# Edge stage: how gathers are released, in what size the one-hot rows are made, and which engine does the small chain steps

## Chip, core, metric

One Trainium2 chip, one of its cores. The metric is device time in microseconds (us) of one execution of the program, the median of three: 3991.97 us (3991.55 to 4013.34). Five engines run their own instruction streams and meet at semaphores: TensorE (PE), VectorE (DVE), ScalarE (ACT), GpSimd (POOL), and SyncE (SP), which here only issues DMAs.

## What is computed

A graph layer over 6250 nodes and 206,250 edges sorted by destination, then attention over all nodes (mix) and eight small expert networks. The change touches only the edge part:

```python
h = (x @ W.T).reshape(n, H, D)                       # 8 heads of 32
alpha = einsum('ehd,hd->eh', h[src], a_src) + einsum('ehd,hd->eh', h[dst], a_dst)
enc = relu(edge_attr @ edge_W.T + edge_b).reshape(-1, H, D)
alpha = alpha + sum(enc * h[dst], axis=-1)
alpha = where(alpha >= 0, alpha, 0.2 * alpha)
amax = segment_max(alpha, dst, num_segments=n)
ex = exp(alpha - amax[dst])
denom = segment_sum(ex, dst, num_segments=n)
out = segment_sum(h[src] * (ex / maximum(denom[dst], 1e-10))[..., None], dst, num_segments=n)
```

## The kernel before

Stages run one after the other: start (node rows, index lists), key/value and mix (both also gather some source rows ahead of time into `scratch_pre_rows`), edges, combine, experts. The edge stage is `stage_edges`. Edges come in groups of 256 (`GE`); a **turn** takes two groups that fall into one block of 64 destination nodes each, 512 edges; there are 452 turns (`D`), and 8 of them (`KW`) make a **window**, for which the maxima of the scores are chained from turn to turn and rescaled. k is a turn's place in its window, 0 to 7.

What a turn d does, and where:

- SP loads the destination rows of its two groups (`table`, ring of `RL` = 3 turns, so turn d's load waits until `spread_out(d - 3)` is done), for every second turn a pair of edge features and of destination numbers repeated on all partitions (`feat`, `relb`: `load_pair(g)` for turns 2g and 2g+1, ring of 2 pairs), and for each window six transfers (`load_window`) and two small ones (`load_turns`). For 124 of the 452 turns, spread evenly, it loads the rows gathered in earlier stages (`is_pre`).
- POOL gathers the source rows of the other 328 turns, four indirect DMAs each, into `rows` (a ring of `R` = 15 turns, free again when the aggregation of turn d - 15 is done).
- DVE makes the one-hot rows `hot` from `relb` (`spreader(d)`, bf16, 128x512), one turn ahead. PE multiplies `table` by them into `ps_d` (`spread_out`), and the features by their weights (`encode`); ACT rectifies the latter (`rectify`), and DVE forms `enc = (enc + a_dst) * ps_d` in two halves (`multiply`). PE sums that by head (`reduce`) into the window's scores `ps_s`.
- Eleven turns later (`LAG`) DVE multiplies the gathered rows by the exponentials (`weigh`), and one turn after that PE aggregates them by destination (`aggregate`), ACT puts the first group's sum back (`put_back`) and DVE adds the second (`add`).
- Once a window, spread over the turns k = 0 to 3 of the next one, the chain: `scores`, two scans, `both_ends`, `chain_runs`, `carry_on`, `fall`, `pick`, `pick_sum`, `lead`, `shift`, then exponentials on ACT (`exponents`, `by_edge`), and, at k = 4, `rescale` on DVE.

Each engine's order is that of the loop `for tau in range(D + LAG + 1)` written out by hand for it. Engines wait only where a line says so. Nothing is reordered at run time: what stands behind a waiting instruction on its engine waits too. In DVE's turn tau the order is `multiply(tau)`, at k = 0 `scores`, then `spreader`, chain pieces, `weigh`, `add`.

## Time and profile before

| | us |
|---|---|
| median of three runs | 3991.97 (3991.55 to 4013.34) |
| the profiled execution, first to last instruction | 4846.5 |
| of it, up to the edge stage | 1040 |
| of it, the edge stage | 2616 |
| of it, combine and experts | 1191 |
| busy in all: PE / DVE / ACT / POOL | 4087.7 / 2700.2 / 2291.3 / 1780.1 |

The profiled execution took 854.5 us longer than the median run. Busy means that an instruction is recorded as running. Ends of matmuls are modelled. A row of a timeline gives start, duration, engine, source line, operation, output<-input, count, and in brackets the idle time of the engine before it and what ended it; "x2" rows merge consecutive instructions of one line.

### The profile page before, as it was taken

How to read it: one execution, taken by the hardware profiler on the slowest of the kernel's cores; microseconds unless marked ns; L12 is line 12 of the kernel's file. 1: busy time of each engine (PE TensorE's matmuls, PEld its weight loads, DVE VectorE, ACT ScalarE, POOL GpSimd, SP SyncE). 2: the span in 40 equal slices, each digit the busy share in tenths (PEclk: the TensorE clock that was granted, in tenths of full speed). 3: DMA queues.
4: the chain of work that ended last, by engine and by line, in shares of the span. 5: the costliest groups of instructions: out<-in, count | busy, mean ns of one | idle time of the engine just before them, and what ended most of it. 6: DMA issues, size and time to landing. Idle time of an engine off the chain costs nothing. (4 is left out here: it accounts for less than half of the span.)

```text
span 4846.5 us, 80424 instructions
## 1 busy us (share of the span) xinstructions
PE 4087.7 (84%) x22764; PEld 1897.1 (39%) x22765; DVE 2700.2 (56%) x5470; ACT 2291.3 (47%) x6074; POOL 1780.1 (37%) x1859
## 2 busy tenths in 40 slices
PE   5699988957888887788887878878887999999999
PEld 3333322312333333333333333333333666666666
DVE  7566723336666666676666666667666333333333
ACT  4444445524555555555555555555554433333332
POOL 3255555644454445444444444445440000000000
PEclk8799989976888888888888887888887799999999
DMA  7555556655555555555555555555552100000000
GB/s 216 160 165 162 164 177 201 210 156 154 161 168 165 158 165 164 162 168 168 159 162 152 163 157 161 162 159 168 164 162 67 61 8 1 8 8 8 8 8 8
DMA packets 378173, 629.74 MB, mean 130 GB/s; under 512 B 83912, under 2 KB 245063, under 8 KB 377536
## 3 DMA queue, kind: packets, MB, share of 16 engines
q1 hardware_dynamic: 277266, 356.80, 23.4%
q0 software_dynamic: 93408, 257.23, 19.5%
q10 hardware_dynamic: 7104, 11.01, 0.7%
q8 instruction: 179, 2.93, 0.2%
q14 instruction: 216, 1.77, 0.1%
HBM read 520.59 MB, written 104.12 MB: 129 GB/s over the span
## 5 line engine op out<-in xcount | busy, mean ns | idle before, releaser
L1629 POOL DMA_INDIRECT s_rows<-scratch_src_rows,s_idx_w x1312 | 1257.6, 959 | 1367.6 <-PE s_ps_a L1692 563.3
L1837 DVE SCALAR_TENSOR_TENSOR s_enc<-s_enc,s_a_dst,s_ps_d 128x512 f32<-128x512 f32 x904 | 634.9, 741 | 313.3 <-DMA p_feats<-in_edge_f,p_tcol_i 160.8
L1734 ACT ACTIVATE s_enc<-s_ps_f 128x1024 f32<-128x1024 f32 x452 | 459.5, 1017 | 516.6 <-remote 265.5
L1692 PE MATMUL s_ps_a<-s_rows,s_hot_e 128*64 128x264 f32 x3616 | 647.1, 490 | 44.9 <-DVE s_rows L1920 32.4
L2285 DVE SCALAR_TENSOR_TENSOR kx_y_all<-e_ps_o,kx_gate,kx_y_all 128x256 f32 (+1 forms) x392 | 173.5, 480 | 684.2 <-PE e_ps_o L2340 684.2
L1920 DVE TENSOR_TENSOR s_rows<-s_rows,s_ps_x 128x1024 f32<-128x1024 f32 x452 | 545.7, 1207 | 13.6 <-ACT s_a_w L1765 8.7
L1688 PE MATMUL s_ps_a<-ke_sums,k_ident 128*128 x790 | 341.0, 520 | 217.1 <-DVE ke_sums L1913 123.6
L1913 DVE TENSOR_TENSOR ke_sums<-s_ps_a,ke_sums 128x264 f32 x509 | 218.3, 429 | 505.3 <-remote 263.9
L1669 PE MATMUL s_ps_s<-s_enc,s_head_sum 128*32 128x256 f32 x3616 | 353.7, 469 | 152.9 <-DVE s_enc L1837 121.2
L1779 ACT ACTIVATE s_hot_e<-k_iota_row,s_rel_w 128x64 f32<-128x64 f32 x1808 | 480.5, 339 | 0.0
L1787 ACT COPY ke_sums<-s_ps_a 128x264 f32 x395 | 148.6, 376 | 552.5 <-remote 337.8
L2299 ACT ACTIVATE ke_sums<-e_ps,kx_b,kx_g 128x448 f32<-128x448 f32 x224 | 162.1, 724 | 512.9 <-PE e_ps L2319 512.9
L1692 PEld LDWEIGHTS s_ps_a<-s_rows,s_hot_e 128*64 128x64 f32 x3616 | 263.0, 163 | 360.2 <-issue 264.5
L2319 PE MATMUL e_ps<-kx_xT,ke_sums 128*128 (+1 forms) x896 | 347.9, 542 | 6.2 <-PEq L180 6.2
L2340 PE MATMUL e_ps_o<-ke_sums 128*128 128x256 f32 x1568 | 347.6, 379 | 0.0
L2329 PE MATMUL e_ps<-ke_sums 128*128 128x448 f32 x896 | 345.9, 539 | 0.0
L1641 PE MATMUL s_ps_f<-s_feat,k_w_rows 30*128 30x512 bf16 x904 | 304.0, 419 | 27.7 <-DMA s_feat<-scratch_step_parts 14.6
L1656 PE MATMUL s_ps_d<-s_hot,s_table 128*128 128x256 bf16 x1808 | 321.7, 308 | 0.0
L2340 PEld LDWEIGHTS e_ps_o<-ke_sums 128*128 128x128 f32 x1568 | 297.7, 190 | 58.6 <-issue 20.9
L1091 POOL DMA_INDIRECT n_rows<-scratch_src_rows,n_idx x248 | 235.0, 947 | 207.0 <-PE n_ps_g L948 107.5
L1195 POOL DMA_INDIRECT m_rows<-scratch_src_rows,m_idx x248 | 235.7, 951 | 174.7 <-issue 64.6
L1688 PEld LDWEIGHTS s_ps_a<-ke_sums,k_ident 128*128 128x128 f32 x790 | 139.0, 220 | 373.5 <-issue 370.6
(280 smaller groups left out, 5259.0 us busy)
## 6 DMA issues: line engine op xcount, KB each, us to landing
s_table<-scratch_dst_parts SPq DMA_DIRECT2D x904, 96.0 KB
s_rows<-scratch_pre_rows SPq DMA_DIRECT2D x124, 528.0 KB
s_relb<-scratch_rel_rows SPq DMA_DIRECT2D x226, 256.0 KB
scratch_pre_rows<-n_rows SPq DMA_DIRECT2D x62, 528.0 KB
scratch_pre_rows<-m_rows SPq DMA_DIRECT2D x62, 528.0 KB
s_rows<-scratch_src_rows,s_idx_w POOLq DMA_INDIRECT x1312
s_feat<-scratch_step_parts SPq DMA_DIRECT2D x226, 54.0 KB
s_pen_w<-scratch_pen_rows SPq DMA_DIRECT2D x228, 48.1 KB
```

The source lines that it names most:

```text
L1629: pool.indirect_dma_start(out=rows[:, d % R, m, :], out_offset=None, in_=scr["src_table"], in_offset=bass.IndirectOffsetOnAxis(ap=idx_w[:, ...
L1656: last = PE.matmul(ps_d[:, c, sub * GE:(sub + 1) * GE], table[:, u, sub, c * P:(c + 1) * P], hot[:, v, sub * GE:(sub + 1) * GE], start=Fal ...
L1669: last = PE.matmul(ps_s[32 * b:32 * (b + 1), :], head_sum[:, 28 - 4 * k:60 - 4 * k], enc[:, d % 2, c, sub * GE:(sub + 1) * GE], start=(k = ...
L1688: PE.matmul(ps_a[:, 0, 0:SRC_W], keep["ident"][:], sums[:, bass.ds(j, 1), :].rearrange("p o w -> p (o w)"), start=True, stop=False, skip_g ...
L1692: last = PE.matmul(ps_a[t * WN:(t + 1) * WN, sub, 0:SRC_W], hot_e[:, d % 3, 2 * sub + t, :], rows[:, d % R, 2 * sub + t, :], start=(sub == ...
L1734: A.activation(enc[:, d % 2], ps_f[:], ACT.Relu).then_inc(enc_made, 1)
L1779: A.activation(hot_e[:, d % 3, m, :], keep["iota_row"][:, 0:WN], ACT.Abs, bias=rel_w[:, w % 3, k * TD + m:k * TD + m + 1]).then_inc(dist_m ...
L1837: V.scalar_tensor_tensor(out=enc[:, d % 2, c, :], in0=enc[:, d % 2, c, :], scalar=a_dst[:, c:c + 1], in1=ps_d[:, c, :], op0=ALU.add, op1=A ...
L1920: V.tensor_tensor(v, v, by.unsqueeze(3).to_broadcast([P, TD, H, HD]), ALU.mult).then_inc(weighed, 1)
L2319: last = nc.tensor.matmul(ps[q][:, 0:W], w["W1"][:, e, c, m * P:(m + 1) * P], keep["xT"][:, c, bass.ds(i * 2 * W + hf * W, W)], start=(c = ...
L2329: last = nc.tensor.matmul(ps[q][:, 0:W], w["W2"][:, e, c, m * P:(m + 1) * P], h1[:, c, hf * W:(hf + 1) * W], start=(c == 0), stop=(c == 1))
L2340: last = nc.tensor.matmul(ps_o[q][:, r, :], h2[:, c, b * P:(b + 1) * P], w["Wo"][:, e, c, :], start=(c == 0), stop=(c == 1))
```

## The change

- One-hot rows: `spreader` now makes both turns of a pair in one instruction, 128x1024, in turns with odd tau, for pair (tau + 3) / 2, so two and three turns ahead (before: one). `hot` has two pairs of buffers; `load_pair` may refill `relb` accordingly earlier. Its place in the sequence of SP stays.
- Chain steps moved from DVE to ACT: the two columns of `first` (`starts`, at k = 1), the copy of the run's end (`keep_run`) and the gap (`fall`, both at k = 2), and the factor of the rescaling (`factors`, at k = 3). DVE waits for `first_made` before it overwrites that pair of `hot`, which is at k = 1.
- `both_ends` is one instruction over 128x32 instead of two over 128x16.
- Gathers: instead of one wait per turn for `enc_made`, each of the 1312 indirect DMAs waits for one event of DVE, three per turn (the first half of `multiply`, a `hot`, a `weigh`), four turns ahead (`LEAD`) on an even pace. The wait for the free slot (`summed`) stays.

```diff
+    LEAD = 4
-        hot = s.sb("hot", [P, 2, ED], BF16)
+        hot = s.sb("hot", [P, 2, 2, ED], BF16)
                 def load_pair(g):
-                    wait(sp, hot_made, 2 * (g - RP + 1))
+                    wait(sp, hot_made, g - RP + 1)
             def _(pool):
+                NG = TD * (D - dims["NP"])
+                def released(g):
+                    tau, part = divmod(3 * g * D // NG - 3 * LEAD, 3)
+                    if part == 0:
+                        wait(pool, prod_made[0], tau + 1)
+                    elif part == 1:
+                        wait(pool, hot_made, (tau + 1) // 2 + 1)
+                    else:
+                        wait(pool, weighed, tau - LAG + 1)
                     wait(pool, summed[1], d - R + 1)
-                    wait(pool, enc_made, d - 4)
                     for m in range(TD):
+                        released(g)
+                        g += 1
 ...
+                def starts(w):
+                    act.wait_ge(hot_made, KW // 2 * w + 1)
+                    wait(act, fac_made, w - 2)
+                    h = hot[:, KW // 2 * w % 2, 0, 0:1]
+                    A.copy(first[:, w % 2, 0:1], h)
+                    A.activation(first[:, w % 2, 1:2], h, ACT.Identity, scale=-1.0, bias=one[:, 0:1]).then_inc(first_made, 1)
+                def keep_run(w):
+                    act.wait_ge(chained, w + 1)
+                    A.copy(runs[:, 1 - u, 0:1], runs[:, u, KS:KS + 1]).then_inc(kept, 1)
+                def fall(w):
+                    act.wait_ge(carry_made, w + 1)
+                    A.activation(gap[:], carry[:, 0:1], ACT.Relu, scale=-1.0, bias=runs[:, w % 2, 2 * KS:2 * KS + 1]).then_inc(gap_made, 1)
+                def factors(w):
+                    act.wait_ge(turned_, w + 1)
+                    A.activation(fac[:], ps_g, ACT.Identity, scale=first[:, w % 2, 0:1], bias=first[:, w % 2, 1:2]).then_inc(fac_made, 1)
 ...
                     if k == 3 and 0 < w <= NW:
+                        if w > 1:
+                            factors(w - 1)
                         by_edge(w - 1)
+                    if k == 1 and tau < D:
+                        starts(w)
 ...
-                def spreader(d):
-                    w, k = win(d)
-                    dve.wait_ge(rel_in[d // 2 % RP], 16 * (d // 2 // RP + 1))
-                    wait(dve, spread[1], d - 1)
-                    V.tensor_scalar(hot[:, d % 2, :], relb[:, d // 2 % RP, d % 2, :], p64[:, 0:1], None, ALU.is_equal).then_inc(hot_made, 1)
-                    if k == 0:
-                        dve.wait_ge(hot_made, d + 1)
-                        V.tensor_copy(first[:, w % 2, 0:1], hot[:, d % 2, 0:1]).then_inc(first_hot, 1)
-                        dve.wait_ge(first_hot, w + 1)
-                        V.tensor_scalar(first[:, w % 2, 1:2], first[:, w % 2, 0:1], -1.0, 1.0, ALU.mult, ALU.add).then_inc(first_made, 1)
+                def spreader(g):
+                    dve.wait_ge(rel_in[g % RP], 16 * (g // RP + 1))
+                    wait(dve, spread[1], 2 * (g - 1))
+                    if g >= 2 and (g - 2) % (KW // 2) == 0:
+                        dve.wait_ge(first_made, (g - 2) // (KW // 2) + 1)
+                    V.tensor_scalar(hot[:, g % 2], relb[:, g % RP], p64[:, 0:1], None, ALU.is_equal).then_inc(hot_made, 1)
 ...
-                    for a, at in ((0, GE - 1), (1, 0)):
-                        last = V.tensor_scalar(ends[:, a, :], turn_of[:, a, :], seg[:, at:at + 1], None, ALU.mult)
-                    last.then_inc(ends_made, 1)
+                    V.tensor_tensor(ends[:], turn_of[:], at, ALU.mult).then_inc(ends_made, 1)
 ...
                 def rescale(w, j):
-                    dve.wait_ge(a_made, w + 1)
-                    V.tensor_scalar(fac[:], ps_g, first[:, w % 2, 0:1], first[:, w % 2, 1:2], ALU.mult, ALU.add).then_inc(fac_made, 1)
 ...
-                    if tau + 1 < D:
-                        spreader(tau + 1)
+                    if tau % 2 == 1 and tau + 3 < D:
+                        spreader((tau + 3) // 2)
```

The order on VectorE, before, from the turn k = 7 of a window into the next turn, k = 0 (`s_hot` are the one-hot rows; L1837 is `multiply`, L1920 `weigh`, L1906 and L1913 `add`):

```order
L1837 SCALAR_TENSOR_TENSOR s_enc<-s_enc,s_a_dst,s_ps_d 128x512 x2
L1826 TENSOR_SCALAR s_hot<-s_relb,s_p 128x512
L1829 CAST s_first<-s_hot 128x1
L1831 TENSOR_SCALAR s_first<-s_first 128x1
L1920 TENSOR_TENSOR s_rows<-s_rows,s_ps_x 128x32x32
L1906 TENSOR_LOAD s_turns_w
L1906 ISA x2
L1913 ISA
L1913 TENSOR_TENSOR ke_sums<-s_ps_a,ke_sums 128x264
L1837 SCALAR_TENSOR_TENSOR s_enc<-s_enc,s_a_dst,s_ps_d 128x512 x2
L1843 TENSOR_TENSOR s_sc<-s_ps_s,s_leak 128x256
L1826 TENSOR_SCALAR s_hot<-s_relb,s_p 128x512
```

The same place after the change:

```order
L1877 SCALAR_TENSOR_TENSOR s_enc<-s_enc,s_a_dst,s_ps_d 128x512 x2
L1871 TENSOR_SCALAR s_hot<-s_relb,s_p 128x1024
L1954 TENSOR_TENSOR s_rows<-s_rows,s_ps_x 128x32x32
L1940 TENSOR_LOAD s_turns_w
L1940 ISA x2
L1947 ISA
L1947 TENSOR_TENSOR ke_sums<-s_ps_a,ke_sums 128x264
L1877 SCALAR_TENSOR_TENSOR s_enc<-s_enc,s_a_dst,s_ps_d 128x512 x2
L1883 TENSOR_TENSOR s_sc<-s_ps_s,s_leak 128x256
L1888 SCALAR_TENSOR_TENSOR s_run_f<-s_pen_w,s_sc 128x256
```

The two rows of `first` are gone, and `hot` at k = 7, now twice as large, is that of the turns k = 2 and 3 of the next window; at k = 0 none is left.

The order on ScalarE after the change, from k = 1 of a window to the start of k = 2 (L1748 is `rectify`, L1822 and L1824 `put_back`, L1759 `take_src`, L1808 `put_exps`):

```order
L1748 ACTIVATE s_enc<-s_ps_f 128x1024
L1822 TENSOR_LOAD s_turns_w
L1822 ISA x2
L1824 ISA
L1824 COPY ke_sums<-s_ps_a 128x264
L1759 COPY s_a_win<-s_rows 128x2x4x4
L1771 CAST s_first<-s_hot 128x1
L1772 ACTIVATE s_first<-s_hot,s_one 128x1
L1808 COPY s_rows<-s_a_w 128x32
L1816 ACTIVATE s_hot_e<-k_iota_row,s_rel_w 128x64 x4
L1818 ACTIVATE s_hot_e<-s_hot_e,s_one 128x256
L1777 COPY s_runs<-s_runs 8x1
```

Of these rows L1771, L1772 and L1777 are new. The two of `first` stand behind `put_back`, which waits for PE's aggregation of the same turn.

## Rows read from the trace of the kernel before

**Rows 1.** Stages: length; busy PE, PEld, DVE, ACT, POOL; clock; DMA share; GB/s.
```profile
1040.00:3656.00 2616.00, 2103.77 (x13210) 844.89 (x13208) 1736.66 (x3307) 1428.12 (x4220) 1255.37 (x1310) 0.81 0.56 161
3656.00:4847.00 1191.00, 1142.02 (x3980) 718.22 (x3980) 420.83 (x1140) 391.30 (x635) 0.00 (x0) 0.95 0.05 17
```

**Rows 2.** DVE instructions by line, 1200 to 3600 us: busy us, mean ns, idle before.
```profile
L1826 DVE TENSOR_SCALAR s_hot<-s_relb,s_p 128x512 bf16<-128x512 bf16 x418 | 149.2, 357 | 0.0
...
L1857 DVE TENSOR_SCALAR s_ends<-s_turn_of,s_seg 128x16 f32<-128x16 f32 x106 | 22.7, 259 | 0.0
...
L1897 DVE TENSOR_SCALAR s_fac<-s_ps_x,s_first 128x8 f32<-128x8 f32 x52 | 14.3, 275 | 0.0
...
L1875 DVE TENSOR_SCALAR s_gap<-s_carry,s_runs 8x1 f32<-8x1 f32 x52 | 10.2, 195 | 0.0
...
L1879 DVE TENSOR_TENSOR s_picked<-s_ps_x,s_turn_of 128x32 f32<-128x32 f32 x52 | 9.5, 183 | 9.6 <-remote 9.4 <-PE s_ps_x L1715 0.3
```

**Rows 3.** DVE's timeline at the turns k = 6 and 7 of one window.
```profile
2419.40 0.34 DVE L1826 TENSOR_SCALAR s_hot<-s_relb,s_p 128x512 bf16<-128x512 bf16 x1
2419.67 1.21 DVE L1920 TENSOR_TENSOR s_rows<-s_rows,s_ps_x 128x1024 f32<-128x1024 f32 x1
...
2423.83 1.40 DVE L1837 SCALAR_TENSOR_TENSOR s_enc<-s_enc,s_a_dst,s_ps_d 128x512 f32<-128x512 f32 x2 [1.61 <-PE s_ps_d L1656]
2425.15 0.34 DVE L1826 TENSOR_SCALAR s_hot<-s_relb,s_p 128x512 bf16<-128x512 bf16 x1
...
2425.79 1.21 DVE L1920 TENSOR_TENSOR s_rows<-s_rows,s_ps_x 128x1024 f32<-128x1024 f32 x1
```

**Rows 4.** SP's queue (DMA issues) in the same turns.
```profile
2411.95 2.69 SPq L1600 DMA_DIRECT2D s_table<-scratch_dst_parts  x2
...
2418.00 0.43 SPq L1575 DMA_DIRECT2D s_rel_w<-scratch_edge_rel  x1
...
2422.94 1.52 SPq L1600 DMA_DIRECT2D s_table<-scratch_dst_parts  x2
...
2425.21 0.43 SPq L1586 DMA_DIRECT2D s_relb<-scratch_rel_rows  x1
```

**Rows 5.** The stage's first relb transfer, as SP issues it.
```profile
1035.67 0.43 SPq L1586 DMA_DIRECT2D s_relb<-scratch_rel_rows  x1
```

**Rows 6.** DVE's first one-hot rows, which waited for that transfer.
```profile
1039.15 0.36 DVE L1826 TENSOR_SCALAR s_hot<-s_relb,s_p 128x512 bf16<-128x512 bf16 x1 [4.07 <-DMA s_relb<-scratch_rel_rows]
```

**Rows 7.** ACT's timeline in a short turn, k = 2.
```profile
2443.64 0.38 ACT L1787 COPY ke_sums<-s_ps_a 128x264 f32 x1 [0.45 <-PE s_ps_a L1692]
2443.91 0.26 ACT L1745 COPY s_a_win<-s_rows 128x32 f32<-128x32 f32 x1
```

**Rows 8.** DVE's multiply of that turn.
```profile
2441.36 1.41 DVE L1837 SCALAR_TENSOR_TENSOR s_enc<-s_enc,s_a_dst,s_ps_d 128x512 f32<-128x512 f32 x2
```

**Rows 9.** Who waited for whom, 2000 to 3000 us: total, times, longest.
```profile
POOL s_rows L1629 <- PE s_ps_a L1692: 215.1, 50, 11.5
...
ACT ke_sums L1787 <- remote: 123.0, 52, 3.7
...
POOL s_rows L1629 <- ACT s_enc L1734: 16.2, 4, 4.7
```

**Rows 10.** POOL's timeline: a gather of the mix stage behind a wait of its own.
```profile
920.83 0.95 POOL L1195 DMA_INDIRECT m_rows<-scratch_src_rows,m_idx  x1 [0.32 <-PE m_ps_n L1221]
```

**Rows 11.** PE's timeline, one turn with k = 3.
```profile
2444.45 0.39 PE L1652 MATMUL s_ps_d<-s_hot,s_table 64*128 64x256 bf16 x4
2444.78 0.61 PE L1656 MATMUL s_ps_d<-s_hot,s_table 128*128 128x256 bf16 x4
...
2447.53 0.71 PE L1722 MATMUL s_ps_x<-s_perm,s_prob 128*128 128x128 f32 x4
...
2448.49 0.64 PE L1669 MATMUL s_ps_s<-s_enc,s_head_sum 128*32 128x256 f32 x8
2449.06 0.39 PE L1652 MATMUL s_ps_d<-s_hot,s_table 64*128 64x256 bf16 x4
```

More of the change, by code:

```diff
@@ L1656, in spread_out @@
                             last = PE.matmul(ps_d[:, c, sub * GE:(sub + 1) * GE], table[:, u, sub, c * P:(c + 1) * P],
-                                             hot[:, v, sub * GE:(sub + 1) * GE], start=False, stop=True, skip_group_check=True)
+                                             hot[:, v, x, sub * GE:(sub + 1) * GE], start=False, stop=True, skip_group_check=True)
                         last.then_inc(spread[c], 1)
@@ L1793, in _ @@
                         leaked(w - 1)
+                    if k == 2 and 0 < w <= NW:
+                        keep_run(w - 1)
+                        fall(w - 1)
                     if k == 3 and 0 < w <= NW:
@@ L1869, in carry_on @@
                     dve.wait_ge(chained, w + 1)
+                    wait(dve, gap_made, w)
                     V.tensor_tensor(carry[:], runs[:, u, 0:2 * KS], chain_w[:, u, 1, :], ALU.add).then_inc(carry_made, 1)
-                    V.tensor_copy(runs[:, 1 - u, 0:1], runs[:, u, KS:KS + 1]).then_inc(kept, 1)
-                def fall(w):
-                    dve.wait_ge(carry_made, w + 1)
-                    V.tensor_scalar(gap[:], carry[:, 0:1], runs[:, w % 2, 2 * KS:2 * KS + 1], 0.0, ALU.subtract, ALU.min).then_inc(gap_made, 1)
                 def pick(w):
@@ L1952, in _ @@
                         back(w - 1)
-                    elif chain == 1:
-                        fall(w - 1)
                     elif chain == 2:
```

16 lines of the change are left out of this document (12 added, 4 removed).

## Prediction

> **What bounds the kernel now.** I read the stages first [rows 1]. The edge stage takes 2616 us of the profiled 4846.5, and DVE is busy for 1736.66 of them. The median run is 3991.97, 854.5 us less than the profiled execution. Combine and experts are filled by PE (1142.02 of 1191), so they have little to give; most of the 854.5 must be missing from stages of many small instructions. If all of it lies in the edge stage, that stage takes 2616 - 854.5 = 1761 us when not profiled, 3.80 us for each of its 464 turns (452 and 12 for the tail), and DVE, with 1737 us of work, is full. The waits agree: the longest of ACT is `put_back`'s, which a row calls remote and not the matmul it really waits for (123.0 us in 52 waits) [rows 9]. Semaphores that come long after the modelled end of a matmul are what a profiled execution would add, and nothing the change can win.
>
> The second look is at PE, to see what DVE may gain before something else ends the turn. One turn at k = 3 runs from 2444.45 to 2449.06, 4.61 us; 0.96 of it (2447.53 to 2448.49) is work that comes once a window, so a plain turn is 3.65 us, and with a quarter of a microsecond a turn for the window's other products about 3.8 [rows 11]. So DVE and PE are both full at about 3.8 us a turn. POOL has 1255.37 us of gathers plus 0.30 between two [rows 1, 10], 1.25 us each: 328 groups of four are 1640 us of 1761. That is close, but not ahead.
>
> **The change on DVE: what it removes, per window of eight turns.**
> - One-hot rows: eight of 357 ns [rows 2] become four. The gap's 8x1 takes 195 ns [rows 2]; from one element to 512 is then 0.16 us, and another 512 cost 0.16 to 0.36 (nothing fixed, or the whole again). I take 0.20. A one-hot row holds DVE only 0.27 us before the next starts (2419.40 to 2419.67) [rows 3], so eight are 2.16 and four larger ones 4 x 0.47 = 1.88: 0.3 saved.
> - `first`: from 2425.15 to 2425.79 is 0.64 us against 0.27 without it [rows 3]: 0.37 saved.
> - The factor: 275 ns and the wait behind it; 0.3. The gap, 195 ns, and the copy of the run's end, of like size, overlap their neighbours: 0.2. Two `ends` of 259 become one of about 190: 0.2 [rows 2].
> - Together 1.4 us a window (0.9 to 1.9), times 56 windows 78 us (50 to 106).
>
> At the one-hot rows a page has another price. The Trainium skill ("VectorE: DVE Perf Modes", the perf-mode tier table) lets a tensor_scalar from SBUF to SBUF in bf16 run at four elements a cycle, which would add 0.13 us for 512 more elements, not 0.20; by it the sum would be 4 x 0.07 x 56 = 16 us better. No row here has the 1024-wide form.
>
> **What it adds, part one: relb.** This is the step I give most weight. SP's order is not changed: the pair for turns 2g, 2g + 1 is loaded behind load(2g - 1), whose tables wait for `spread_out(2g - 4)`. Before, DVE read it at turn 2g - 1, three turns later. Now it reads it in turn 2g - 3, right behind `multiply`, one turn later. A relb transfer issued at 1035.67 [rows 5] let DVE start at 1039.15 [rows 6]: 3.5 us. In most turns that fits (one turn and a multiply are 3.8 + 1.3 = 5.1; the two tables before it take 1.5). It does not fit once a window, for the pair of k = 2 and 3, which DVE wants at k = 7. Before this one SP also issues the window's six transfers: table pair 1.52, then 2418.00 to 2422.94, then 2422.94 to 2425.21 [rows 4], 1.52 + 4.94 + 2.27 = 8.7 us from the release by `spread_out` at k = 5, and 3.5 for the transfer, 12.2 us. DVE wants it two turns and a multiply after that product: 2 x 3.80 + 1.32 = 8.9, and later by as much as PE runs ahead. PE can be ahead by what DVE has left of its turn after multiply (3.80 - 1.40 = 2.40) less `reduce` (0.57) and both products (0.9) [rows 11], so by at most about 0.9. That leaves 12.2 - 9.8 = 2.4 us. SP's issues are drawn out in the profiled execution as well, I take off 0.9: 1.5 us a window. The ends are 0 (SP a third faster, a quicker landing) and 3.5. The trace itself shows the upper one: relb was issued at 2425.21 [rows 4], when the one-hot row of k = 7 had started at 2425.15 [rows 3]. What is queued behind: weigh, the add and the next multiply, all of DVE, and PE by its `reduce`.
>
> **Part two: first_made.** DVE's one-hot rows at k = 1 now wait for two ACT instructions of the same turn, which stand behind `put_back`. In a short turn ACT started `take_src` at 2443.91 [rows 7], 2.55 us after DVE's multiply began at 2441.36 [rows 8]; the two new ones end some 0.5 later, 3.05, while DVE is free after 1.32. That is 1.7 us of wait, less up to 0.9 if PE is ahead. I take 0.7 (0 to 1.7); behind it stand the chain, weigh and the add of k = 1.
>
> **Part three, small.** `factors` runs on ACT before `by_edge`, for which `weigh` at k = 3 waits: 0.15 us. ACT gets five instructions a window, none longer than `take_src`'s 0.26 [rows 7], about 1 us of 30; it is busy for 1428 of 1761 us [rows 1] and takes it.
>
> **The gathers: nothing.** The removed wait (for `rectify`) ended 4 waits of POOL in 1000 us, 16.2 us; the one that stays (the slot, freed by PE's aggregation) ended 50, 215.1 us [rows 9]. The new events lie four to two turns ahead of the turn gathered, the slot comes free three turns ahead, in the middle of the turn; so the slot goes on deciding. In the mix stage gathers already wait one by one, and one with a wait of its own started 0.32 us after the last [rows 10], against 0.30 elsewhere. Bound: 0 to 0.02 x 1312 = 26 us of POOL time, which has 120 to spare. A wait that did bind would hold POOL, and then `take_src` on ACT and `rectify` behind it.
>
> **The sum.** Per window -1.4 + 1.5 + 0.7 + 0.15 = +0.95 us; times 56 = +53 us. On the profiled execution's own time that is 4846.5 + 53 = 4899.5; on the median 3991.97 + 53 = 4045. The median is 0.82 of the span, but the terms are not scaled by that: they are instruction durations and a transfer, and the pace that I compared them with is the unprofiled one.
>
> **Rivals.**
> - *relb is in time.* If SP is faster by more than 2.4 us over those eleven issues, only first_made is left and can shrink as well. Then -1.4 + 0.2 = -1.2, times 56: 3925. For it: the 4.94 us contain a turn read by SP that may be stretched. Against: six issues remain, and a transfer needs its 3.5 us. This case lies on the other side; it decides where the waits add up to less than 1.4 us a window.
> - *PE sets the turn.* If PE needs 3.8 and DVE after the change 3.6, the saving is worth nothing and stalls of 1.5 to 2 us a window are made up in turns in which DVE has less to do. 3992, within 30. For it: rows 11. Against: both stalls lie at k = 7 and 1, around k = 0 and 2, where DVE has scans and shifts and no time to make up.
> - *Stalls in full.* 3.5 + 1.7 + 0.15 - 1.4 = 3.95, times 56: 4213. For it: the trace's own times at k = 7 and 2. Against: they are profiled times.
> - *The gathers' events bind after all*, POOL falls behind and each turn that it gathers for is late. 30 us or more slower; rows 9 and 10 speak against it.
>
> **Chances and range.** Slower by one to four per cent, stalls larger than savings: 0.46, with the full stalls and the gathers in it. relb in time: 0.30. PE, or an even sum, within 1%: 0.24. About 1% is what a measurement of this kernel can tell from no change. The range reaches from a little below the rival at 3925, since savings could be 1.9 a window (3886), to 4150, under the full stalls: 3900 to 4150. The forecast's own range is 4033 to 4150.
>
> **What would show it.** In the profile after: DVE's one-hot rows as 226 instructions of about 0.5 us, with idle time before them that is ended by the relb transfer, some 56 times 1.5 to 3.5 us at k = 7, and by ACT's `first` at k = 1; before, there was none (0.0 at L1826 [rows 2]). POOL's waits should still be for PE's aggregation. DVE busy in the edge stage should fall by 50 to 106 us from 1736.66. It is wrong if the one-hot rows show no idle time, or if POOL waits mostly for DVE's events; and if idle time is there and the kernel is still faster, then DVE was not the engine that set the turn.

## The result: the change makes the kernel 10% slower

The kernel after the change takes 4419.67 us (median of four runs, 4410.92 to 4424.87), the kernel before, run beside it, 3994.64 us. The ratio is 1.1044 (95% interval 1.102 to 1.1069): 425 us are lost. The prediction said 4045, in a range of 3900 to 4150. Its direction and its two waits are there; the size is eight times the one predicted.

From the page of the profile after: the span, the busy time of each engine, the clock granted to PE in 40 slices, and the group of instructions that matters (line, engine, operation, output<-input, count | busy us, mean ns | idle time before them and what ended most of it).

```profile
span 4409.1 us, 80138 instructions
PE 3843.5 (87%) x22765; PEld 1838.4 (42%) x22765; DVE 2604.2 (59%) x4903; ACT 2358.7 (53%) x6358; POOL 1787.1 (41%) x1859
PEclk8799899958989888888989888888976999999999
...
L1871 DVE TENSOR_SCALAR s_hot<-s_relb,s_p 128x1024 bf16<-128x1024 bf16 x226 | 113.4, 502 | 453.9 <-DMA s_relb<-scratch_rel_rows 352.3
```

The last row is the result: the 226 one-hot instructions stood behind 453.9 us of idle VectorE time, 352.3 of it ended by the `relb` transfer; the smaller ones of before stood behind 0.0 [rows 2]. What grew is idle time: VectorE is busy for less than before (2604.2 us; `b_again`, the kernel before on a chip of the same sort, has 2675.9), and PE for more (3843.5 against 3671.2), at a lower granted clock (0.901 against 0.946 in the mean).

The waits of the kernel after, 1800 to 2800 us (engine, instruction <- what it waited for: us in total, times, longest), to be read beside [rows 9]:

```profile
POOL s_rows L1643 <- PE s_ps_a L1706: 214.6, 57, 9.0
...
DVE s_hot L1871 <- DMA s_relb<-scratch_rel_rows: 146.1, 47, 6.7
...
POOL s_rows L1643 <- DVE s_rows L1954: 70.2, 31, 6.6
...
DVE s_hot L1871 <- ACT s_first L1772: 45.1, 23, 3.4
```

GpSimd still waits for PE's aggregation most, as predicted. Its waits for `weigh` are new, and the experiments below ask whether they are a cause or a consequence.

One thing must be told before any number is compared. The 854.5 us between the profile that the prediction read and the median run are not the price of profiling. The execution of the kernel after that gave the profile took 4410.92 us, with a span of 4409.1, beside 4417.99 to 4424.87 for the other three; and the kernel before, profiled again as `b_again`, has a span of 3993.7. The chips differ. Unchanged, the kernel before took 3994.42 to 3998.92 us on three chips used here, and 4778.66 to 4788.66 on three others. The trace that the prediction read (4846.5) came from a chip of the second sort, the times that it was made for from the first. Every ratio below is to the kernel before on the same chip. Differences in us between kernels are taken within one chip where both ran there; `a_again` and `a_both_early` ran on another chip than the four `h_` kernels, and the kernel before took 3994.42 us on the one and 3997.49 on the other.

### The profile page after: what moved, and what is told of

It reads as the page before. It is cut to its first block and busy times, and to the rows that moved or that the text cites. A ratio compares the mean times of both kernels' runs of the same rounds, so it can differ in the third digit from the quotient of the medians.

```text
span 4409.1 us, 80138 instructions
## 1 busy us (share of the span) xinstructions
PE 3843.5 (87%) x22765; PEld 1838.4 (42%) x22765; DVE 2604.2 (59%) x4903; ACT 2358.7 (53%) x6358; POOL 1787.1 (41%) x1859
## 5 line engine op out<-in xcount | busy, mean ns | idle before, releaser
L1706 PE MATMUL s_ps_a<-s_rows,s_hot_e 128*64 128x264 f32 x3616 | 606.4, 464 | 7.7 <-DVE s_rows L1954 7.3
L1702 PE MATMUL s_ps_a<-ke_sums,k_ident 128*128 x790 | 329.9, 505 | 297.7 <-DVE ke_sums L1947 257.5
L1748 ACT ACTIVATE s_enc<-s_ps_f 128x1024 f32<-128x1024 f32 x452 | 460.3, 1018 | 206.9 <-PE s_ps_f L1655 197.8
L1824 ACT COPY ke_sums<-s_ps_a 128x264 f32 x395 | 149.8, 379 | 598.1 <-PE s_ps_a L1706 598.0
L1871 DVE TENSOR_SCALAR s_hot<-s_relb,s_p 128x1024 bf16<-128x1024 bf16 x226 | 113.4, 502 | 453.9 <-DMA s_relb<-scratch_rel_rows 352.3
L1706 PEld LDWEIGHTS s_ps_a<-s_rows,s_hot_e 128*64 128x64 f32 x3616 | 251.0, 156 | 303.4 <-issue 214.9
L1683 PE MATMUL s_ps_s<-s_enc,s_head_sum 128*32 128x256 f32 x3616 | 327.8, 438 | 34.9 <-DVE s_enc L1877 33.0
L1702 PEld LDWEIGHTS s_ps_a<-ke_sums,k_ident 128*128 128x128 f32 x790 | 134.7, 214 | 438.9 <-issue 435.9
L1655 PE MATMUL s_ps_f<-s_feat,k_w_rows 30*128 30x512 bf16 x904 | 280.8, 391 | 12.7 <-DMA s_feat<-scratch_step_parts 12.7
L1670 PE MATMUL s_ps_d<-s_hot,s_table 128*128 128x256 bf16 x1808 | 291.2, 286 | 0.0
```

Of the source, the lines that this page charges most:

```text
L1670: last = PE.matmul(ps_d[:, c, sub * GE:(sub + 1) * GE], table[:, u, sub, c * P:(c + 1) * P], hot[:, v, x, sub * GE:(sub + 1) * GE], start= ...
L1683: last = PE.matmul(ps_s[32 * b:32 * (b + 1), :], head_sum[:, 28 - 4 * k:60 - 4 * k], enc[:, d % 2, c, sub * GE:(sub + 1) * GE], start=(k = ...
L1702: PE.matmul(ps_a[:, 0, 0:SRC_W], keep["ident"][:], sums[:, bass.ds(j, 1), :].rearrange("p o w -> p (o w)"), start=True, stop=False, skip_g ...
L1706: last = PE.matmul(ps_a[t * WN:(t + 1) * WN, sub, 0:SRC_W], hot_e[:, d % 3, 2 * sub + t, :], rows[:, d % R, 2 * sub + t, :], start=(sub == ...
L1748: A.activation(enc[:, d % 2], ps_f[:], ACT.Relu).then_inc(enc_made, 1)
```

## Experiments

### First chip: four parts alone

Four kernels, on a chip on which the kernel before took 4788.66 us. One loads `relb` a pair earlier in SP's order; `load_feat` holds the other half of the old `load_pair` and keeps its place.

```
a_relb_early, against the kernel after:
+                    if d == 0:
+                        load_rel(0)
                     if d % 2 == 0:
-                        load_pair(d // 2)
+                        if d // 2 + 1 < D // 2:
+                            load_rel(d // 2 + 1)
+                        load_feat(d // 2)
a_first_k0, against the kernel after:
-                    if k == 1 and tau < D:
+                    if k == 0 and tau < D:
                         starts(w)
b_pairs, against the kernel before (first stays on VectorE):
-        hot = s.sb("hot", [P, 2, ED], BF16)
+        hot = s.sb("hot", [P, 2, 2, ED], BF16)
-                    if tau + 1 < D:
-                        spreader(tau + 1)
+                    if tau % 2 == 1 and tau + 3 < D:
+                        spreader((tau + 3) // 2)
b_gathers, against the kernel before (hot event: wait(pool, hot_made, tau + 2)):
-                    wait(pool, enc_made, d - 4)
                     for m in range(TD):
+                        released(g)
+                        g += 1
```

> The changed kernel with one edit: SP issues each relb transfer one pair (two turns) earlier in its order; features stay. Theory 1 (DVE's one-hot rows wait for relb, 352 us in the profile of the changed kernel, and that is most of the loss): the wait for relb goes to under 30 us, the kernel takes 4420 - 352 = about 4070 us, still above 3995 by what the wait for first costs. Rival (the transfer is late because the DMA engines are fuller, not because it is issued late; or other waits take its place): over 4250 us, or the wait for relb stays.

> The changed kernel with one edit: ACT makes the two columns of first at k = 0 instead of k = 1, a turn before DVE needs them. Theory 1 (the wait costs what the profile shows, 45.1 us per 1000, about 100 us in the stage): 4320 us. Rival (the wait stands in front of the relb wait or runs beside PE's work, so that its end only brings the next wait forward): 4400 us or more.

> The kernel before with one part of the change alone: one-hot rows of two turns at once, two and three turns ahead, relb loaded at SP's old place; first stays on DVE, gathers as before. Theory 1 (relb lateness makes most of the loss by itself): 3995 + 350 - 20 saved = about 4325 us, with waits of DVE for relb as in the changed kernel. Rival (the loss comes from the combination with gathers or ACT steps): under 4100 us.

> The kernel before with another part alone: each gather waits for one event of DVE (multiply, one-hot rows, weigh; three a turn, four turns ahead). The prediction's step (these events are long past when a slot is free): within 1% of before, 3955 to 4035 us, POOL waits for PE's aggregation. Rival (paced gathers spread the DMA load and help, or bind and hurt): outside of that.

| kernel | us | ratio to before (95% interval) |
|---|---|---|
| a_relb_early | 4821.13 | 1.0075 (1.0037 to 1.0114) |
| a_first_k0 | 4854.27 | 1.0137 (1.0105 to 1.017) |
| b_pairs | 4849.93 | 1.0137 (1.0098 to 1.0176) |
| b_gathers | 4776.73 | 0.9974 (0.9951 to 0.9997) |

The gathers' events cost nothing. Each expected time here was meant for a chip of the other sort, so only the waits can be compared with the expectations: VectorE's idle time for `relb` falls from 253.7 us in `a_first_k0` to 4.2 in `a_relb_early`, and that for `first` from 160.5 in `a_relb_early` to none. Nothing else here comes near 10%, neither alone nor as the rest of the change. So either the loss was an interaction of parts, or it does not exist on a chip like this one. The next runs tell that apart.

### Both kernels again, unchanged, and both repairs at once

On a chip on which the kernel before took 3994.42 us: `b_again` (one execution) and `a_again` are the two kernels with no edit, `a_both_early` is the kernel after with the edits of `a_relb_early` and `a_first_k0` together.

> The kernel before, unchanged, profiled again beside the others, so that its rows and those of the changed kernel come from one chip. Theory (the profile of before was taken where semaphores arrive late, and that makes up the 854 us between it and the median): where it takes about 3995 us, PE's semaphores come within 0.1 us of the matmuls' ends and no wait is called remote; where it takes about 4800 they come 1 us late and more. Rival (profiling itself stretches this kernel): over 4800 in either case.

> The changed kernel, unchanged, beside the kernel before on the same chip. If the loss of 10% belongs to the change alone, 1.10 times before again on any chip; if it belongs to the change on a chip without late semaphores (there the turn is short, and a late relb has nothing to hide behind), 1.10 where before takes about 3995 us and 1.01 to 1.02 where it takes about 4800 us.

> The changed kernel with relb issued one pair earlier and first made at k = 0 on ACT, so with neither of the two new waits of DVE's one-hot rows. Theory 1 (these two waits are the whole loss, and the saving on DVE is real): on a chip where before takes 3995 us, 3995 - 80 = 3915 us; where it takes 4790, about 4770. Rival (gathers' events or ACT's new work cost too): over 4050 us on the first kind of chip.

`b_again` took 3995.49 us, `a_again` 4401.14 (ratio 1.1018, 1.0972 to 1.1064), `a_both_early` 3919.48 (0.9812, 0.9771 to 0.9853). With the transfer issued a pair earlier and `first` made a turn earlier the whole loss is gone, and the kernel is 1.9% faster than before.

The tile `s_hot` in the three traces (duration in ns, least / median / most; first and last start; then what ended the idle time before it, us and times). Of `b_again`:

```profile
L1826 DVE TENSOR_SCALAR s_hot<-s_relb,s_p x452: 334/346/539, 885.8 to 2789.1; 128x512 bf16<-128x512 bf16 x151
...
  DMA s_relb<-scratch_rel_rows: 4.4, 2
```

Of `a_again`:

```profile
L1871 DVE TENSOR_SCALAR s_hot<-s_relb,s_p x226: 477/486/729, 884.1 to 3183.0; 128x1024 bf16<-128x1024 bf16 x113
...
  DMA s_relb<-scratch_rel_rows: 338.7, 103
  ACT s_first L1772: 101.8, 54
```

Of `a_both_early`:

```profile
L1878 DVE TENSOR_SCALAR s_hot<-s_relb,s_p x226: 472/479/670, 884.1 to 2704.4; 128x1024 bf16<-128x1024 bf16 x113
...
  DMA s_relb<-scratch_rel_rows: 4.2, 1
```

The first and last starts give the pace of the stage. The first starts agree within 2 us, so all that differs is in the turns. From the first to the last of the 226 are 225 pairs: (3183.0 - 884.1) / 450 = 5.11 us a turn in `a_again`, and (2704.4 - 884.1) / 450 = 4.05 in `a_both_early`. For before it is (2789.1 - 885.8) / 451 = 4.22. The 4.2 to 4.4 us of `relb` that stay in two of them are the stage's start.

VectorE's idle time for `relb` and `first` in `a_again` is 338.7 + 101.8 = 440.5 us. The two kernels differ by 4401.14 - 3919.48 = 481.7; where the rest is, the corrected sum below tells.

### Where in the window the time goes

From the starts of `multiply` in the timelines I worked out the mean length of a turn for each k (from one start to the next, us, without the first three windows and the last, incomplete one):

| k | 0 | 1 | 2 | 3 | 4 | 5 | 6 | 7 | sum |
|---|---|---|---|---|---|---|---|---|---|
| b_again | 4.82 | 4.98 | 4.64 | 4.05 | 4.29 | 3.56 | 3.65 | 3.65 | 33.6 |
| a_again | 5.22 | 5.57 | 5.40 | 5.34 | 3.61 | 4.02 | 3.69 | 8.01 | 40.9 |
| a_both_early | 4.61 | 4.39 | 4.38 | 4.61 | 3.60 | 3.40 | 3.66 | 3.65 | 32.3 |

Of the 7.2 us that a window loses, 4.4 are at k = 7, where the prediction had put its main wait. There VectorE's timeline in one window of `a_again`, one of the longer waits, reads as follows (start, us, engine, line, instruction, count, in brackets the idle time before it and what ended it); the three `multiply` rows are those of k = 6, 7 and 0:

```profile
2188.62 1.39 DVE L1877 SCALAR_TENSOR_TENSOR s_enc<-s_enc,s_a_dst,s_ps_d 128x512 f32<-128x512 f32 x2
...
2192.02 1.41 DVE L1877 SCALAR_TENSOR_TENSOR s_enc<-s_enc,s_a_dst,s_ps_d 128x512 f32<-128x512 f32 x2 [0.54 <-PE s_ps_d L1670]
2199.48 0.49 DVE L1871 TENSOR_SCALAR s_hot<-s_relb,s_p 128x1024 bf16<-128x1024 bf16 x1 [6.06 <-DMA s_relb<-scratch_rel_rows]
2199.88 1.21 DVE L1954 TENSOR_TENSOR s_rows<-s_rows,s_ps_x 128x1024 f32<-128x1024 f32 x1
2201.01 0.42 DVE L1947 TENSOR_TENSOR ke_sums<-s_ps_a,ke_sums 128x264 f32 x1
```

And SP's queue in front of it, from the features of the pair k = 0 and 1 of the next window on. The tables of k = 0, the window's six transfers (L1576, L1580, L1582), the tables of k = 1 and the two small ones of `load_turns` stand ahead of the `relb` transfer, twelve issues in all:

```profile
2182.59 0.77 SPq L1589 DMA_DIRECT2D s_feat<-scratch_step_parts  x1
2184.62 1.47 SPq L1601 DMA_DIRECT2D s_table<-scratch_dst_parts  x2
2186.13 1.52 SPq L1576 DMA_DIRECT2D s_rel_w<-scratch_edge_rel  x1
2187.69 2.88 SPq L1580 DMA_DIRECT2D s_pen_w<-scratch_pen_rows  x4
2190.61 0.47 SPq L1582 DMA_DIRECT2D s_chain_w<-scratch_chain  x1
2192.10 1.49 SPq L1601 DMA_DIRECT2D s_table<-scratch_dst_parts  x2
2193.64 0.32 SPq L1570 DMA_DIRECT2D s_turns_w<-scratch_turns  x1
2194.00 0.35 SPq L1572 DMA_DIRECT2D s_idx_w<-scratch_edge_idx  x1
2194.40 0.42 SPq L1587 DMA_DIRECT2D s_relb<-scratch_rel_rows  x1
```

PE had finished the product of k = 5 at 2183.39 (its row starts at 2182.78 and is 0.61 long); the row at 2192.59 is of k = 7, the last two are of k = 0:

```profile
2182.78 0.61 PE L1670 MATMUL s_ps_d<-s_hot,s_table 128*128 128x256 bf16 x4
...
2192.59 0.71 PE L1702 MATMUL s_ps_a<-ke_sums,k_ident 128*128 x2
...
2196.16 0.60 PE L1655 MATMUL s_ps_f<-s_feat,k_w_rows 30*128 30x512 bf16 x2
2201.69 1.24 PE L1702 MATMUL s_ps_a<-ke_sums,k_ident 128*128 x2 [4.93 <-DVE ke_sums L1947]
```

On the prediction's path the lengths in this window are: from the product of k = 5 to the first table 2184.62 - 2183.39 = 1.23 us; from there to `relb` 2194.40 - 2184.62 = 9.78; from issue to use 2199.48 - 2194.40 = 5.08; together 16.1. VectorE was through with `multiply` at 2192.02 + 1.41 = 2193.43, 10.04 us after the product. The difference, 6.1, is the wait of 6.06.

This window is not a typical one: the issue at 2186.13 took 1.52 us, the longest of its kind, and 0.43 in the median. The means over the 56 windows of `a_again`, beside the prediction's numbers:

| us | predicted | mean of 56 | this window |
|---|---|---|---|
| product of k = 5 to first table | 0 | 0.8 | 1.23 |
| first table to `relb` issue | 8.7 | 9.3 | 9.78 |
| issue to use | 3.5 | 4.2 | 5.08 |
| needed | 12.2 | 14.3 | 16.1 |
| product of k = 5 to the end of `multiply` of k = 7 | 9.8 | 9.65 | 10.04 |
| wait | 1.5 (2.4 less 0.9) | 4.7 | 6.06 |

The product of k = 5 is also not what SP waits for. In the code the read of the turn's number stands ahead of that wait, and SP comes late to both: in 43 of the 56 windows it had begun the read before the product ended, and the profile's semaphores show it waiting for the product in at most 6. Here SP works without a break from 2179.95, when the product of k = 4 let it issue the tables of k = 7, to the `relb` issue at 2194.40. The queue is full; it is its own length that makes the transfer late.

Over all windows, the `relb` transfer of this pair was issued a median of 2.2 us after `multiply` of k = 7 began and took 4.3 us (median) from issue to use, and VectorE waited a median of 4.8 us there.

PE shows what stands behind it: it worked ahead up to 2196.76 and then stood idle for 4.93 us until VectorE's `add`. Its next two products at L1702 took 1.24 us where the last two of the same shape had taken 0.71.

The wait at k = 7 comes in all 56 windows and makes 262 of the 338.7 us (4.7 a window in the mean). The pairs wanted at k = 3 and k = 5 are in time in the median, but one in three is over 0.5 us late and one in ten about 2 us; they add 59 us. Some 15 us lie ahead of the first turn, where the first two pairs are waited for (4 in the kernel before), and 2 at one k = 1. In all `relb` costs 338.7 / 56 = 6.0 us a window, with the start in it.

The same transfer was just as late before, and it did no harm. SP's `relb` issue in one window of `b_again`, and VectorE's turn k = 7:

```profile
1966.45 0.42 SPq L1586 DMA_DIRECT2D s_relb<-scratch_rel_rows  x1
```

```profile
1964.29 1.41 DVE L1837 SCALAR_TENSOR_TENSOR s_enc<-s_enc,s_a_dst,s_ps_d 128x512 f32<-128x512 f32 x2 [0.43 <-PE s_ps_d L1656]
1965.61 0.53 DVE L1826 TENSOR_SCALAR s_hot<-s_relb,s_p 128x512 bf16<-128x512 bf16 x1
```

`relb` was issued at 1966.45, 2.16 us after this `multiply` began, much as in `a_again` (2.2 in the median). The one-hot row at 1965.61 was that of the next turn and did not need it; the one that did came two turns later, 7.5 us (median) after the issue.

The wait for `first`, at k = 1 of `a_again`, is where the prediction had it too:

```profile
1959.81 1.41 DVE L1877 SCALAR_TENSOR_TENSOR s_enc<-s_enc,s_a_dst,s_ps_d 128x512 f32<-128x512 f32 x2 [1.08 <-PE s_ps_d L1670]
1963.04 0.48 DVE L1871 TENSOR_SCALAR s_hot<-s_relb,s_p 128x1024 bf16<-128x1024 bf16 x1 [1.82 <-ACT s_first L1772]
```

### Why the first chip did not show it

The same kernels were then timed on another chip of the slower sort (before: 4782.18 us), to see whether the first chip was one of a kind. `f_relb_early`, `f_pairs` and `f_both_early` have the edits shown; `f_both_oldg` is `f_both_early` with the gathers' waits of before:

```
-                        released(g)
-                        g += 1
+                    wait(pool, enc_made, d - 4)
```

> The changed kernel with relb alone issued one pair earlier (the same edit as in a_relb_early, again, for a chip on which before takes about 3995 us). The relb wait was 147.9 us per 1000, 2300 us of stage: 340 us; the wait for first stays, 43.3 per 1000. Theory 1: 4400 - 340 = 4060 us, less what PE gains from a higher granted clock, so 4000 to 4060. Rival (waits hide each other): over 4100 us.

> The kernel before with the one-hot rows of two turns at once alone (the same edit as in b_pairs, again, for such a chip): relb late, first on DVE, gathers as before. Theory 1 (late relb by itself): 3995 + 340 - 20 = about 4315 us, turns with k = 7 about 8 us long. Rival (the gathers' new waits are needed for the loss): under 4150 us.

> The changed kernel with relb one pair earlier and first at k = 0, again, now in three rounds: 3915 to 3925 us, 0.98 of before, where before takes about 3995 us. Rival: the earlier ratio of 0.981 came from one pair of executions and moves by over 0.5%.

> As f_both_early, but with the gathers' waits of the kernel before. The prediction's step (the gathers' events change nothing): within 0.3% of f_both_early. Rival (even pacing of gathers is worth something on its own): over 0.3% slower than f_both_early.

| kernel | us | ratio to before (95% interval) |
|---|---|---|
| f_relb_early | 4820.65 | 1.0071 (1.0046 to 1.0097) |
| f_pairs | 4832.03 | 1.0101 (1.0038 to 1.0165) |
| f_both_early | 4763.16 | 0.9953 (0.9931 to 0.9974) |
| f_both_oldg | 4767.96 | 0.997 (0.9942 to 0.9998) |

These chips agree with each other. What differs on them is how long after a matmul the engine that waits for it starts. Two timelines show it on the same instructions: PE's aggregation (eight matmuls, two groups of four in one row) and ScalarE's `put_back`, which waits for the first four. In the trace that the prediction read:

```profile
2437.52 1.64 PE L1692 MATMUL s_ps_a<-s_rows,s_hot_e 128*64 128x264 f32 x8
2440.13 0.38 ACT L1787 COPY ke_sums<-s_ps_a 128x264 f32 x1 [2.51 <-remote]
```

In `b_again`:

```profile
1941.85 1.11 PE L1692 MATMUL s_ps_a<-s_rows,s_hot_e 128*64 128x264 f32 x8
1942.65 0.38 ACT L1787 COPY ke_sums<-s_ps_a 128x264 f32 x1 [1.57 <-PE s_ps_a L1692]
```

In `b_again` `put_back` starts 0.8 us after the first matmul, before all eight have ended. In the other trace it starts 0.97 us after the last of the eight. Over the whole edge stage the semaphore of the aggregation was updated a median of about 1.4 us after the modelled end of the matmul in that trace (1.3 to 1.55, by how updates and matmuls are paired), and 0.02 us after it in `b_again` and `a_again`. In the other traces from these chips it is between 0.6 and 1.5 us. The ends of matmuls are modelled, so a late semaphore and a late end look alike; but from the last product with `hot` to the end, where PE is nearly full, the one trace has 1195 us (3651.2 to 4846.5) and `b_again` 1202 (2791.4 to 3993.7), so the matmuls are not slower in that stretch. The idle times that rows call "remote" are only on the slower chips: 123.0 us in 1000 before [rows 9], and none in the waits of `b_again`.

On these chips a mean turn of the kernel before takes 5.74 us; SP then has two turns and a multiply of about 13 us and not of 9 to 10, and much of what is still late falls into a time in which VectorE waits for PE in any case. The waits of `b_pairs`, 2000 to 3000 us:

```profile
DVE s_hot L1826 <- DMA s_relb<-scratch_rel_rows: 89.6, 38, 7.2
```

The wait for `relb` is there, 258.5 us in the whole stage, and the kernel is only 61 us slower (4849.93 against 4788.66). On the chips with early semaphores the same kernel loses 283 us with 338.5 of idle time (below); some 55 us come back there, about 22 of them in VectorE's busy time (2654.0 us against 2675.9 in `b_again`) and the rest in its other waits. With as much coming back here, over half of the wait took the place of others. The whole change was not run unedited on a chip of this sort; the kernel after with one of the two repairs, and the pairs alone, cost 0.7 to 1.4% here. Why the semaphores come late on some chips no run here tells.

### The parts, on a chip with early semaphores

With that known, the four parts were run on a chip on which the kernel before took 3997.49 us: the edits shown above, and `h_oldg`, which is `a_both_early` with the gathers' waits of before.

> The changed kernel with relb alone issued one pair earlier. Where before takes about 3995 us: the relb wait (147.9 us per 1000, 340 us in the stage) is gone and the wait for first (1.7 us a window, 98 us) stays: 3919 + 98 = about 4015 us. Rival (the waits hide each other): over 4100 us. Where before takes about 4790 us: 1.007 of it, as measured.

> The kernel before with the paired one-hot rows alone, relb late. Where before takes about 3995 us: 3995 + 340 - 20 = about 4315 us. Rival (the gathers' new waits are needed for the loss): under 4150 us. Where before takes about 4790 us: 1.01 of it.

> The changed kernel with first at k = 0 alone. Where before takes about 3995 us: 4400 - 98 = about 4300 us if the waits add up; over 4370 us if the time goes to the next relb wait. Where before takes about 4790 us: 1.014 of it.

> Both waits away, gathers with the waits of before. Where before takes about 3995 us: 3919 us within 0.3% if the gathers' events are worth nothing, 3935 us or more if even pacing is worth something. Where before takes about 4790 us: 0.997 of it.

| kernel | us | ratio to before (95% interval) | idle for relb / first, us |
|---|---|---|---|
| a_again | 4401.14 | 1.1018 (1.0972 to 1.1064) | 338.7 / 101.8 |
| h_first_k0 | 4278.94 | 1.0714 (1.0661 to 1.0767) | 364.2 / 0 |
| h_pairs | 4280.43 | 1.0717 (1.0649 to 1.0785) | 338.5 / 0 |
| h_relb_early | 4049.98 | 1.014 (1.009 to 1.0191) | 3.9 / 123.6 |
| a_both_early | 3919.48 | 0.9812 (0.9771 to 0.9853) | 4.2 / 0 |
| h_oldg | 3925.45 | 0.9829 (0.977 to 0.9887) | 4.1 / 0 |

The last column is from the tile `s_hot` of each trace. Its rows in `h_relb_early` and in `h_first_k0`:

```profile
  ACT s_first L1779: 123.6, 54
```

```profile
  DMA s_relb<-scratch_rel_rows: 364.2, 125
```

Alone, each wait costs what it is long. Against `a_both_early`, `h_first_k0` loses 359 us with 364.2 of idle time, and `h_relb_early` loses 130 with 123.6. Taking the `relb` wait out of the kernel after gains 351 us, taking `first` out 122, and both 482: they add up within 9 us. `h_relb_early` is 35 us over its expected 4015, in part since the wait for `first` grew to 123.6 when the other was gone. The pairs alone, put into the kernel before, lose 283 of the 406 us.

The gathers' events are within 6 us of the old waits (3919.48 and 3925.45 on two chips, 4763.16 and 4767.96 on one), with intervals of the ratios that overlap. GpSimd's new waits for `weigh` (70.2 us in 1000 after the change) are thus what the stalls leave behind and no cause: when the stalls go, they add nothing that can be measured.

### Moving the window's transfers instead

If SP's queue is the cause, then a shorter queue ahead of this `relb` helps k = 7, but the six transfers will delay another pair. The window's load goes from k = 0 to k = 2 of SP's order; the kernel is otherwise the one after.

```
w_window_k2 and x_window_k2, against the kernel after:
-                    if k == 0:
+                    if k == 2:
                         load_window(w)
w_pairs_early: b_pairs with the SP order of a_relb_early
```

> The changed kernel with one edit: SP issues the six window transfers two turns later, behind the relb of k = 2 and 3 instead of in front of it. Theory (these six, 4.9 us of issuing, make that relb late): the wait at k = 7 falls from 4.8 us to under 1.5, and part of it comes up at k = 1, where the next relb now stands behind them; as that one had 2 us more, 4400 - 56 x 3 = about 4230 us. Rival (relb is late by the transfer's own 4 us, whatever is in front): the wait at k = 7 stays over 3 us and the time over 4350. Where before takes about 4790 us only the wait at k = 7 can be read.

> The kernel before with paired one-hot rows and relb one pair earlier: the part without its late transfer. The sum had 0.3 us a window saved, 17 us: 3978 us where before takes 3995. Rival (the wider instruction saves as much as half of each, 0.13 us x 4 more): 3950 us.

> The edit of w_window_k2 again: the six window transfers behind the relb of k = 2 and 3. Where before takes about 3995 us: the wait at k = 7 falls from 4.8 us to under 2, the wait at k = 1 (1.7 us now, for first) grows, about 4230 us; rival: the wait at k = 7 stays over 3 us, over 4350 us.

On a chip with late semaphores (before: 4778.66 us), `w_window_k2` took 4865.26 us (1.0173, 1.0114 to 1.0232); its idle time for `relb` at k = 7 is 32 us in all, against 184 in `a_first_k0`. `w_pairs_early` took 4777.84 (1.0006, 0.9983 to 1.0029), against 1.0137 and 1.0101 for the pairs with `relb` in its old place. So the longer one-hot rows alone gain nothing that can be measured on such a chip; the 17 us expected of them were not tested on one of the other sort. On a chip with early ones (before: 3998.92) `x_window_k2` took 4290.96 (1.0734, 1.0688 to 1.078). The tile `s_hot` in it:

```profile
  DMA s_relb<-scratch_rel_rows: 295.2, 136
  ACT s_first L1772: 50.2, 22
```

The turn k = 7 shrinks from 8.01 to 5.30 us, and k = 1 grows from 5.57 to 6.69, since the pair wanted there now stands behind the six transfers; VectorE is idle 3.0 us there (median). The wait at k = 7 fell to 1.7 us (median), as expected, but the kernel gained 110 us and not 170: more than foreseen came up at k = 1. So the wait moved with the transfers, as a queue would have it, and most of it stayed: the pair needs its lead, not a better neighbour.

## Why the prediction was wrong

**Direction, place and mechanism were right.** The wait for `relb` is at k = 7, behind `multiply`, ended by the transfer that SP issues behind the window's six; the wait for `first` is at k = 1. Undoing the one gives back 351 us, the other 122.

**The step that failed: the term for relb.** It was 12.2 us needed, less 8.9 + 0.9 available, less 0.9: 1.5 us a window. In the mean of the 56 windows the time available was 9.65 us, so that part was right. The time needed was 14.3, and three parts of it were too small:
- *The deduction of 0.9 us* for SP's issues being drawn out in a profiled execution. The issues are no shorter elsewhere: the window's six take 3.86 us (median) both in the trace that the prediction read and in `b_again`.
- *SP's own work.* The step let SP start at the product of k = 5 and gave it 8.7 us (it spoke of eleven issues; they are twelve). SP was late there already, by 0.8 us in the mean, since it had not stopped issuing; and the issues took 9.3.
- *The transfer.* One transfer, the stage's first [rows 5, 6], gave 3.5 us. Under the load of the stage it is 4.2 in the mean.

These are 0.9 + 0.8 + 0.6 + 0.7 = 3.0 us, and with 0.15 less available the whole way from 1.5 to 4.7.

The median wait at k = 7 is 4.8 us. Even the prediction's upper end for this wait, 3.5, which the trace before seemed to show, was below it.

**And it happens more than once a window.** The step said that it fits in most turns. In the median it does, but the pairs wanted at k = 3 and 5 are late often enough to add 1.1 us a window, and the start of the stage adds 0.3: 6.0 us and not 4.7.

**The term for first: 0.7 predicted, 1.8 measured** (101.8 / 56; the median wait is 1.7). The working gave 1.7 and took off 0.9 for a lead of PE. VectorE waits here for ScalarE, which is behind `put_back` and so behind PE; so a lead of PE does not shorten it, and 1.7 would have been right.

**The reading of the 854.5 us failed, with less harm.** The prediction laid them to profiling and put them all into the edge stage, which gave 3.80 us a turn. They are a difference of chips; about 153 of them lie ahead of the stage (its first one-hot rows start at 885.8 us in `b_again`, at 1039.15 before [rows 6]), and a turn of `b_again` is 4.22. But this reading is what made the stalls look like something to be trimmed: the deduction for SP's issues and the sentence against the rival of stalls in full ("they are profiled times") come from it, and the lead of PE was worked out with its 3.80. The rival stood at 4213; even that was some 190 us too low, mostly since it had the wait at k = 7 at 3.5 us and none at k = 3 and 5.

**Right: VectorE's saving.** Predicted 1.4 us a window (0.9 to 1.9), and 50 to 106 us less of VectorE's busy time; the pages of `b_again` and `a_again` have 2675.9 and 2603.9. With both waits gone the kernel gains 3995 - 3919 = 76 us, 1.35 a window, and the rival with `relb` in time was 3925. In the price of the longer one-hot row the part for 512 more elements was too high: a row takes 486 ns against 346, so 0.14 us and not 0.20. The Trainium skill ("VectorE: DVE Perf Modes", the perf-mode tier table) lets such an instruction run at four bf16 elements a cycle; an estimate from that is 0.13, and these rows agree with it.

**Half right: what sets the turn.** The gain is not spread over the window. The table of turns has it at k = 0, 1, 2, 4 and a little at 5; k = 3 is longer by 0.56 us. At k = 6 and 7 a turn takes 3.65 us in `b_again` and 3.65 to 3.66 in `a_both_early`; PE is busy for all of it in both, and VectorE for 0.87 and 0.96 of it before, 0.81 and 0.91 after. There the rival "PE sets the turn" holds, with the plain turn of 3.65 us that the prediction read [rows 11].

**Right: the gathers. Too low: the load on ScalarE.** The events cost nothing. The moved steps are short (`first` 193 and 295 ns, the factor 357, the gap 290 in `a_both_early`), but `weigh` waits longer for the exponentials that `by_edge` writes, behind `factors`: 22.3 us before, 42.6 in `a_again` and 41.5 in `a_both_early`, while `h_pairs`, in which ScalarE has no new step, has 19.7. That is 0.35 us a window and not 0.15. VectorE's waits of 880 to 3250 us in `b_again` and in `a_again`:

```profile
DVE ke_sums L1913 <- PE s_ps_a L1692: 44.2, 39, 3.6
...
DVE s_rows L1920 <- ACT s_a_w L1765: 22.3, 54, 1.4
```

```profile
DVE ke_sums L1947 <- PE s_ps_a L1706: 69.1, 62, 3.6
DVE s_rows L1954 <- ACT s_a_w L1802: 42.6, 46, 1.7
```

**The sum, corrected.** From `b_again` to `a_again` VectorE is busy 72 us less and waits 436 us more in front of its one-hot rows, 20 more in front of `weigh` and 25 more in front of `add`, for PE's aggregation: 409 us. Measured are 406. Per window that is -1.3 + 7.8 + 0.35 + 0.45.

The wait in front of `add` is in no term of the prediction, and the clock has a part in it. Stretches of 900 to 2700 us (length, busy of PE, PEld, DVE, ACT, POOL, granted clock, DMA share, GB/s) in `b_again`, `a_again` and `a_both_early`:

```profile
900.00:2700.00 1800.00, 1676.31 (x12528) 716.59 (x12520) 1625.57 (x3135) 1372.52 (x4003) 1203.99 (x1243) 0.96 0.77 222
```

```profile
900.00:2700.00 1800.00, 1517.06 (x10303) 618.14 (x10300) 1287.24 (x2144) 1165.79 (x3506) 985.38 (x1024) 0.87 0.64 183
```

```profile
900.00:2700.00 1800.00, 1707.56 (x13002) 736.07 (x12999) 1612.43 (x2703) 1461.36 (x4432) 1250.05 (x1289) 0.98 0.80 230
```

The granted clock is 0.87 with the stalls and 0.96 to 0.98 without. PE falls to its lower level (0.50 of full speed, 1.2 GHz against 2.4) behind such a stall. Around the one at k = 7 shown above, the granted clock was 1.00 up to 2196 and 0.50 in the 1.5 us after the stall:

```profile
2190.00:2196.00 6.00, 6.00 (x56) 2.69 (x50) 2.88 (x5) 5.08 (x17) 4.48 (x6) 1.00 0.57 162
2201.50:2203.00 1.50, 1.31 (x4) 0.64 (x6) 1.50 (x3) 0.00 (x0) 0.00 (x0) 0.50 0.72 238
```

It falls again behind the wait for `first`. PE's aggregation of k = 1 and of k = 2 of that window, and the `add` of k = 2:

```profile
2207.93 1.11 PE L1706 MATMUL s_ps_a<-s_rows,s_hot_e 128*64 128x264 f32 x8
...
2214.18 2.03 PE L1706 MATMUL s_ps_a<-s_rows,s_hot_e 128*64 128x264 f32 x8
```

```profile
2216.37 0.43 DVE L1947 TENSOR_TENSOR ke_sums<-s_ps_a,ke_sums 128x264 f32 x1 [0.99 <-PE s_ps_a L1706]
```

The same eight matmuls took 0.92 us longer, and VectorE waited 0.99 us for them. In `a_again` 34.7 us of the wait in front of `add` are at k = 2, where the granted clock is 0.72 in the mean; in `a_both_early` none is, and the clock there is 1.00. How much of the 25 us the lower clock makes, and how much PE's coming late out of the stall, is not shown; no run held the clock apart from the stalls.

## What to carry to other kernels

A reader moved ahead in its own engine's order needs its loads moved ahead as well: count from the release of the load to the use, with everything that its queue does in between, register reads too, and at the point of the period where the queue has most to do; and look whether the queue waits at that release at all, or comes to it late. A wait that a trace shows in full stands in the sum in full, until a second trace shows it shorter; and when the profile's span is far from the times, ask first whether the two come from the same chip. Here, on a chip with early semaphores, each stall of VectorE alone was paid for in full (359 us lost for 360 more of idle time, 130 for 123), though PE sets some of the turns.

## What the hardware showed that I had not expected

- Chips differ by 20% on the same program (3994 to 3999 us and 4779 to 4789). What differs in the traces is how long after a matmul's modelled end its semaphore is updated: a median of 0.02 us, and of about 1.4 us in the trace of the kernel before. The paired one-hot rows alone cost 7.2% on the one sort and 1.0 to 1.4% on the other.
- A stall of 5 us once in 41 us, with the smaller ones beside it, goes with a granted clock of 0.87 over the stage and not 0.96, and what PE runs right behind the stall goes at half speed.
- A one-hot row over 1024 elements takes 0.486 us, one over 512 0.346.
- A `relb` transfer takes 4.3 us from issue to use in the median where the queues are busy; the stage's first took 3.5 in the trace before.
